# Latent attention taken two heads at a time, with zero-filled rows, a reordered end and an early table load

## The reference

```python
c_q = h_t @ W_DQ + b_DQ
c_kv = h_t @ W_DKV + b_DKV
q_c = (c_q @ W_UQ + b_UQ).reshape(b, s, N_HEADS, D_K).transpose(0, 2, 1, 3)
k_c = (c_kv @ W_UK + b_UK).reshape(b, s, N_HEADS, D_K).transpose(0, 2, 1, 3)
v_c = (c_kv @ W_UV + b_UV).reshape(b, s, N_HEADS, D_K).transpose(0, 2, 1, 3)
q_r = (c_q @ W_QR + b_QR).reshape(b, s, N_HEADS, D_HR).transpose(0, 2, 1, 3)
k_r = (h_t @ W_KR + b_KR)[:, None, :, :]
...
scores = jnp.einsum('bhsd,bhtd->bhst', q, k) * scale
attn = jax.nn.softmax(scores, axis=-1)
o = jnp.einsum('bhst,bhtd->bhsd', attn, v_c)
o = o.transpose(0, 2, 1, 3).reshape(b, s, N_HEADS * D_K)
return o @ W_O + b_O
```

## Time and profile before

| | us |
|---|---|
| median of 3 runs | 893.99 (893.89 to 899.29) |
| profiled execution | 893.57 |
| its span, first to last instruction | 891.9 |
| TensorE busy in the span | 858.8 |
| attention: latent down projection's copies to the last addition | 150.3 to 212.9 |

### The profile page before, as it was taken

The page is one execution under the profiler, slowest core; times in us unless marked ns, Lnnn a source line. Parts: engine busy times, 40 slices in busy tenths (PEclk is TensorE's granted clock), DMA queues, the critical chain, the costliest instruction groups (busy, mean ns, idle before and its releaser), DMA issues.

```text
span 891.9 us, 19675 instructions
## 1 busy us (share of the span) xinstructions
PE 858.8 (96%) x6818; PEld 524.5 (59%) x6818; DVE 595.4 (67%) x1534; ACT 491.3 (55%) x935; POOL 420.2 (47%) x394
## 2 busy tenths in 40 slices
PE   8999999999999999889999999999999999889998
PEld 7888887557567656644444444444444444567656
DVE  2476555664523222878888888888888888379875
ACT  3344443551112122678888888888888888632010
POOL 1332222000241010168888888888888888522000
PEclk9999999999999999999999999999999999999999
DMA  7944497904515613896566655566655562710220
GB/s 241 299 172 161 169 364 279 337 6 154 163 44 83 119 37 140 233 267 137 77 90 88 85 76 76 69 87 87 85 76 76 70 88 96 126 48 1 49 49 24
DMA packets 78391, 109.86 MB, mean 123 GB/s; under 512 B 27036, under 2 KB 64544, under 8 KB 74307
## 3 DMA queue, kind: packets, MB, share of 16 engines
q1 hardware_dynamic: 73019, 93.70, 48.5%
q0 software_dynamic: 4960, 14.96, 4.5%
q10 hardware_dynamic: 360, 0.50, 0.3%
HBM read 86.29 MB, written 21.06 MB: 120 GB/s over the span
## 4 chain that ended last, share of the span: by engine, by line
PE 84%; DVE 7%; SPq 3%; issue 2%; DMA 2%; ACT 2%; ACTq 0%; POOL 0%; DVEq 0%
PE bank L1538 15%; PE bank L1565 14%; PE bank L1512 7%; PE bank L1391 6%; PE bank L1194 5%; PE bank L1181 5%; PE bank L1550 4%; PE bank L1419 3%; PE bank L1800 3%; PE bank L1359 2%; PE bank L1147 2%; PE bank L1277 2%; PE bank L1268 2%; PE bank L1860 2%; SPq L500 1%
## 5 line engine op out<-in xcount | busy, mean ns | idle before, releaser
L759 POOL TENSOR_TENSOR region<-region 128x512 int32<-128x512 int32 x256 | 321.4, 1276 | 61.0 <-ACT region L1042 61.0
L1042 ACT ACTIVATE region<-bank 128x512 f32<-128x512 f32 x512 | 279.6, 596 | 59.9 <-PE bank L1550 48.0
L2287 DVE CUSTOM_DVE_ANT_0 xnT<-bank,region 128x1024 bf16<-128x1024 f32 x128 | 156.1, 1220 | 51.9 <-issue 51.4
L1538 PE MATMUL bank<-region 128*128 (+1 forms) x1024 | 158.5, 276 | 7.7 <-ACT region L1024 5.2
L2287 DVE CUSTOM_DVE_ANT_0 region<-bank,region 128x1024 bf16<-128x1024 f32 x128 | 156.1, 1220 | 0.0
L1538 PEld LDWEIGHTS bank<-region 128*128 128x128 bf16 x1024 | 79.7, 100 | 112.9 <-ACT region L1042 65.2
L1565 PE MATMUL bank<-region 128*32 128x256 f32 x2048 | 139.7, 387 | 0.0
L1565 PEld LDWEIGHTS bank<-region 128*32 128x32 f32 x2048 | 59.1, 109 | 46.9 <-issue 15.6
L706 POOL DMA_DIRECT2D keys_split<-region x48 | 35.8, 748 | 98.2 <-DVE region L2052 98.2
L1512 PE MATMUL bank<-region,xnT 64*128 64x512 bf16 x244 | 73.5, 381 | 0.0
L1514 PE MATMUL bank<-region,xnT 64*128 64x512 bf16 x244 | 73.5, 381 | 0.0
(11 more groups left out here) (395 smaller groups left out, 1324.3 us busy)
## 6 DMA issues: line engine op xcount, KB each, us to landing
region<-keys_split SPq DMA_DIRECT2D x224, 128.0 KB, 5.0
region<-in_ctx SPq DMA_DIRECT2D x32, 512.0 KB, 7.4
keys_split<-region POOLq DMA_DIRECT2D x48, 256.0 KB, 4.1
region<-in_L_ffn_we_gate SPq DMA_DIRECT2D x8, 688.0 KB
region<-in_L_ffn_we_up SPq DMA_DIRECT2D x8, 688.0 KB
region<-in_mask_1x1xSxS_ik SPq DMA_DIRECT2D x1, 4096.0 KB, 16.5
region<-in_L_ffn_we_down SPq DMA_DIRECT2D x8, 512.0 KB
mask_kept<-region SPq DMA_DIRECT2D x1, 2048.0 KB, 9.4
```

Source lines behind the costliest of these rows:

```text
L759: nc.gpsimd.tensor_tensor(out=bits, in0=bits, in1=keep4[k], op=ALU.mult).then_inc(probs_kept, 1)
L1042: nc.scalar.activation(prob4[n % PROBS].rearrange("p a b -> p (a b)"), bank[:, SCORE4[n], :], ACT.Exp, scale=SCALE4).then_inc(exp4_ready, 1)
L1538: last = mm(bank[:, SCORE4[n], k * S:(k + 1) * S], slab[s][:, t * P:(t + 1) * P], qT4[:, bass.ds(u, 1), :].rearrange("p o q -> p (o q)"), ...
L2287: v.tensor_tensor_reduce(out=junk[q], in0=bank[:, 3 + 2 * q:5 + 2 * q, :].rearrange("p a b -> p (a b)"), in1=maskN[:, q, 2 * c * CH:2 * (c ...
```

## The change

Units are numbered anew: a step takes two heads of one batch (`unit2`), so four units are heads 0 and 1 of batch 0, then of batch 1. Rows 65 to 127 of `kvr` and `uT2` and rows 33 to 127 of `cq1` and `fold2` are cleared (GpSimd and ScalarE, near the program's start), and queries and scores multiply all 128 rows. `values2` takes both heads of a step alternately. `TURN2` and `MASKS2` say in which step queries are made and masks turned. VectorE copies turned probabilities a step later than before. At the end, latent outputs are copied per batch, and the first batch's output product comes before the last value products. An exponential of one element on ScalarE makes the table of exponentials load before the down projection's copies.

```diff
 SCORE2 = (6, 7, 4)
+STEPS2 = UNITS2 // 2
+TURN2 = ((2, 3), (), (4, 5), (), (6, 7), (), (), ())
+MASKS2 = ((), (0, 1), (), (2, 3), (), (4, 5), (6,), (7,))
+def unit2(n):
+    return n // 4 * 2 + n % 2, n // 2 % 2
...
             nc.gpsimd.memset(zeros, 0.0).then_inc(setup, 1)
             pool.wait_ge(setup, 4)
+            nc.gpsimd.memset(kvr[COLS2 - 1:P, :], 0.0)
+            nc.gpsimd.memset(cq1[ROWS2 - 1:64, :], 0.0)
+            nc.gpsimd.memset(cq1[64:P, :], 0.0)
+            nc.gpsimd.memset(fold2[ROWS2 - 1:64, :, :], 0.0)
+            nc.gpsimd.memset(fold2[64:P, :, :], 0.0).then_inc(row_blank, 1)
+            pool.wait_ge(row_blank, 1)
             nc.gpsimd.memset(kvr[COLS2 - 1:COLS2, :], 1.0).then_inc(setup, 1)
             pool.wait_ge(setup, 5)
...
                 act.wait_ge(fold2_psum, 2)
+                for r in range(2):
+                    nc.scalar.activation(uT2[r][64:P, :].rearrange("p (a b) -> p a b", b=P),
+                                         ones[64:P, :].unsqueeze(1).broadcast_to([64, T // P, P]), ACT.Copy, scale=0.0)
+                act.wait_ge(row_blank, 1)
                 kept = bank[0:ROWS2, 5, 0:H2 * ROWS2].rearrange("p (h c) -> p h c", c=ROWS2)
                 nc.scalar.activation(fold2[0:ROWS2, :, 0:DCQ], kept[:, :, 0:DCQ], ACT.Copy, scale=SCALE2)
...
+            act.wait_ge(setup, 2)
+            nc.scalar.activation(small[0:1, 7:8], half[0:1, 0:1], ACT.Exp)
             act.wait_ge(in_w2, 16 * N_W2)
             act.wait_ge(setup, 6)
...
-            def values_out(g):
-                act.wait_ge(o2_psum, UNITS2 // 2 * (g + 1))
-                nc.scalar.activation(oT2[:, g, :], bank[:, 5 if g == 0 else 2, :], ACT.Copy).then_inc(o2_ready, 1)
+            def values_out(g, n, c):
+                act.wait_ge(o2_psum, n)
+                nc.scalar.activation(oT2[:, g, c], bank[:, 5 if g == 0 else 2, c], ACT.Copy).then_inc(o2_ready, 1)
             queries_out(0)
             queries_out(1)
             exps(0)
-            for n in range(UNITS2):
-                if n + 1 < UNITS2:
-                    exps(n + 1)
-                if n % 2 == 1 and (n + 3) // 2 < H2:
-                    queries_out((n + 3) // 2)
-                if n % 2 == 0:
-                    mask_out(n // 2)
-                if n == UNITS2 // 2 + 1:
-                    values_out(0)
-            values_out(1)
+            exps(1)
+            for i in range(STEPS2):
+                if i == 0:
+                    queries_out(TURN2[0][0])
+                if i + 1 < STEPS2:
+                    exps(2 * i + 2)
+                for h in TURN2[i][:1] if i else ():
+                    queries_out(h)
+                for g in MASKS2[i][:1]:
+                    mask_out(g)
+                if i + 1 < STEPS2:
+                    exps(2 * i + 3)
+                for h in TURN2[i][1:]:
+                    queries_out(h)
+                for g in MASKS2[i][1:]:
+                    mask_out(g)
+                if i == STEPS2 // 2 + 1:
+                    values_out(0, UNITS2 // 2, slice(0, T))
+            values_out(1, UNITS2 - 2, slice(0, S))
+            values_out(1, UNITS2, slice(S, T))
...
             def queries2(h):
                 pe.wait_ge(u2_ready, h)
-                if h > 1:
-                    pe.wait_ge(maskT_ready, h - 1)
-                mm(bank[0:COLS2, 3, :], fold2[0:ROWS2, h, :], cq1[0:ROWS2, :], start=True, stop=True)\
+                if h >= 4:
+                    pe.wait_ge(maskT_ready, h // 2 * 2 - 2)
+                mm(bank[0:COLS2, 3, :], fold2[:, h, :], cq1, start=True, stop=True)\
                     .then_inc(u2_psum, 1)
             def mask_T(g):
-                pe.wait_ge(u2_ready, min(g + 2, H2))
-                if g > H2 - 2:
+                pe.wait_ge(u2_ready, min(g // 2 * 2 + 4, H2))
+                if g > 0:
...
             def scores(n):
-                h, b = n // B, n % B
+                h, b = unit2(n)
                 if b == 0:
                     pe.wait_ge(u2_ready, h + 1)
                 if n >= 3:
                     pe.wait_ge(exp2, n - 2)
                 for q in range(QT):
                     t = b * S + q * P
-                    last = mm(bank[:, SCORE2[n % 3], q * S:(q + 1) * S], uT2[h % 2][0:COLS2, t:t + P],
-                              kvr[0:COLS2, b * S:(b + 1) * S], start=True, stop=True)
+                    last = mm(bank[:, SCORE2[n % 3], q * S:(q + 1) * S], uT2[h % 2][:, t:t + P],
+                              kvr[:, b * S:(b + 1) * S], start=True, stop=True)
                 last.then_inc(score2, 1)
-            def values2(n):
-                h, b = n // B, n % B
-                r = 32 * (h % 4)
-                pe.wait_ge(pT2_ready, n + 1)
+            def probs_T(n):
+                pe.wait_ge(norm2, n + 1)
+                if n >= 2:
+                    pe.wait_ge(pT2_ready, n - 1)
                 for k in range(2):
-                    last = mm(bank[r:r + DCQ, 5 if h < 4 else 2, b * S:(b + 1) * S], ckv[:, b * QT + k, :],
-                              pT2[n % 2][:, k, :], start=(k == 0), stop=(k == 1), skip_group_check=True)
-                last.then_inc(o2_psum, 1)
+                    for q in range(QT):
+                        last = nc.tensor.transpose(bank[:, n % 2, k * S + q * P:k * S + (q + 1) * P],
+                                                   p2[n % RING2][:, q, k * P:(k + 1) * P], ident[:, :])
+                last.then_inc(pT2_psum, 1)
+            def values2(i):
+                pe.wait_ge(pT2_ready, 2 * i + 2)
+                for k in range(2):
+                    for n in (2 * i, 2 * i + 1):
+                        h, b = unit2(n)
+                        r = 32 * (h % 4)
+                        last = mm(bank[r:r + DCQ, 5 if h < 4 else 2, b * S:(b + 1) * S], ckv[:, b * QT + k, :],
+                                  pT2[n % 2][:, k, :], start=(k == 0), stop=(k == 1), skip_group_check=True)
+                        if k == 1:
+                            last.then_inc(o2_psum, 1)
             pe.wait_ge(cq_ready, 1)
-            mm(bank[0:COLS2, 3, :], fold2[0:ROWS2, 0, :], cq1[0:ROWS2, :], start=True, stop=True).then_inc(u2_psum, 1)
+            mm(bank[0:COLS2, 3, :], fold2[:, 0, :], cq1, start=True, stop=True).then_inc(u2_psum, 1)
             pe.wait_ge(kvr_ready, 1)
             for t in range(TT):
                 last = nc.tensor.transpose(bank[:, 5, t * DCQ:(t + 1) * DCQ], kvr[0:DCQ, t * P:(t + 1) * P],
...
-            for n in range(UNITS2):
-                if n + 2 < UNITS2:
-                    scores(n + 2)
-                if n % 2 == 1 and (n + 3) // 2 < H2:
-                    queries2((n + 3) // 2)
-                if n % 2 == 0:
-                    mask_T(n // 2)
-                pe.wait_ge(norm2, n + 1)
-                if n >= 2:
-                    pe.wait_ge(pT2_ready, n - 1)
-                for k in range(2):
-                    for q in range(QT):
-                        last = nc.tensor.transpose(bank[:, n % 2, k * S + q * P:k * S + (q + 1) * P],
-                                                   p2[n % RING2][:, q, k * P:(k + 1) * P], ident[:, :])
-                last.then_inc(pT2_psum, 1)
-                if n > 0:
-                    values2(n - 1)
-            values2(UNITS2 - 1)
-            pe.wait_ge(o2_ready, 2)
+            for i in range(STEPS2):
+                if i + 1 < STEPS2:
+                    scores(2 * i + 2)
+                    if i > 0:
+                        scores(2 * i + 3)
+                for h in TURN2[i][:1]:
+                    queries2(h)
+                if i == 0:
+                    scores(3)
+                for g in MASKS2[i][:1]:
+                    mask_T(g)
+                if i > 0:
+                    values2(i - 1)
+                for h in TURN2[i][1:]:
+                    queries2(h)
+                probs_T(2 * i)
+                probs_T(2 * i + 1)
+                for g in MASKS2[i][1:]:
+                    mask_T(g)
             for t in range(TT):
+                if t == QT:
+                    values2(STEPS2 - 1)
+                if t % QT == 0:
+                    pe.wait_ge(o2_ready, 2 + t // QT)
                 for g in range(2):
...
                                 AX.X, ALU.max, negate=True).then_inc(nmax2, 1)
-            max2(0)
-            max2(1)
-            for n in range(UNITS2):
+            def norm_probs(n):
                 s = n % RING2
                 dve.wait_ge(exp2, n + 1)
                 link(v.reciprocal(sm2[s][:, 2, :], sm2[s][:, 1, :]))
                 v.tensor_tensor(p2[s], p2[s], sm2[s][:, 2, :].unsqueeze(2).broadcast_to([P, QT, S]), ALU.mult)\
                  .then_inc(norm2, 1)
-                if n + 2 < UNITS2:
-                    max2(n + 2)
+            def probs_out(n):
                 dve.wait_ge(pT2_psum, n + 1)
                 if n >= 2:
-                    dve.wait_ge(o2_psum, n - 1)
+                    dve.wait_ge(o2_psum, n // 2 * 2)
```

(15 more changed lines are left out.)

## The result

The changed kernel took 882.35 us (median of four runs, 881.08 to 886.77) where the kernel before, beside it, took 893.94 (four, 893.11 to 899.29). The ratio is 0.9857, 95% interval 0.9815 to 0.9900; times 893.94 that is 881.2. The profiled execution took 881.08 with a span of 879.4, so 12.49 less than the 893.57 of before. From the start of the copy of the latent keys on VectorE to the end of the second addition ("the attention" from here on) it was 62.54 us before and is 52.22 now.

The account below looks back on a forecast made before the run. TensorE was taken to bound the latent attention, each head costing its matmuls in order, 6.83 us. Gains of 0.3, 6.8 and 3.3 sum to 10.4; 893.57 less that gives 883.2 us, range 881.5 to 888.5.

Parts of the forecast that it names:

- start of the attention to the maximum of unit 4: Head of the latent attention: earlier first maximum and shorter first steps bring unit 4's maximum from 163.45 to 163.15, gain 0.3 us.
- units 4 to 14: Middle of the latent attention: three mask and two query steps take 27.31 us in place of 34.12, gain 6.8.
- end: From unit 14's maximum to the end of the second addition: 11.95 us in place of 15.28, gain 3.3.
- Zero rows: Attention's queries and scores over 128 rows: queries take 0.86 us in place of 1.00, scores neither gain nor lose.
- Values in pairs: Two heads' value products in two column groups overlap: eight records take 0.98 us for two units in place of 1.96.
- Pairs in program order: Rival on value products: strict matmul order needs five slots, not four, 0.22 us more per step; 883.8 us, chance 0.05.
- No overlap of the pairs: Rival on value products: TensorE needs 6.1 us a step and binds again; gain 5.5, time 888.1 us, chance 0.11.
- The ring: VectorE and ScalarE bind the attention's steps: 5.65 us in mask steps, 5.18 in query steps, 4.69 with neither.
- Joints stay: Rival on TensorE's array-form changes: it binds at the old group lengths, 5.85 us a step; 885.2 us, chance 0.10.
- Steps no longer overlap: Rival on attention steps: VectorE's copies wait for the same step's turnings, 8.4 us a step; 898.1 us, chance 0.02.
- End, table, clearing: Attention's end takes 11.95 us from unit 14's maximum; early table load gains 0.15 within the head's 0.3; clearing is hidden.
- the drain of 1.38: Rival on ScalarE's early table load: draining first starts the queries 0.5 us late; 883.7 us, chance 0.02.

Follow-up runs that it names:

- the two runs above: Changed kernel with one head's value products waiting for the end of the other's, 889.97 us; and with values written unit after unit without that wait, 881.59 us.
- the nine kernels of the table: Kernel before, before with zero rows, and changed kernels with 33/65, 33 or 65 rows, serial values, copies between maxima, mask pieces, late table; cross attention 404.07 to 404.21 us.
- before again: Kernel before, unchanged, profiled a second time: 900.39 us, attention 69.83 us, cross attention 403.78 us.
- the second comparison: Both kernels run again unchanged: changed kernel 883.0 us (six runs) against 898.83 us for the kernel before (eleven runs), ratio 0.9831.

## Why the prediction was right about the mechanism and short by two microseconds

The profiled executions can be compared with the working term by term:

| term | predicted | measured |
|---|---|---|
| start of the attention to the maximum of unit 4 | 0.3 | 0.22 (0.79 less the 0.57 by which it started earlier) |
| units 4 to 14 | 6.8 | 34.12 - 27.30 = 6.82 |
| end | 3.3 | 15.28 - 12.01 = 3.27 |
| ahead of the attention | 0 | 0.57 |
| behind it | 0 | 1.58 |

*Zero rows:* right on the joints. Queries gain (0.62 in the changed kernel, 1.95 over sixteen units of the old one), scores have the large form already.

*Values in pairs:* right, 1.06 for eight records against 0.98 to the next group; *Pairs in program order* and *No overlap of the pairs* fall with the two runs above.

*The ring:* right, mask steps 5.66 against 5.65, query steps 5.15 against 5.18. The margin of 0.1 that it left TensorE held for the first maximum alone: behind a query step the second starts 0.83 after the first in place of 0.60, which is hidden because ScalarE still has the first pair of exponentials and the mask copies to do. *Joints stay* falls, since TensorE idles in the steps; *Steps no longer overlap* falls, since the copies don't wait.

*End, table, clearing:* 12.01 against 11.95 from the maximum of unit 14; the load is followed at once, as in the earlier trace rows, so the drain of 1.38 that the Trainium skill ("ScalarE: Activation LUTs", What ACT_TABLE_LOAD costs) adds is not seen here either: 147.64 + 1.28 = 148.92, and the next row starts at 148.93. The root did not move.

**The step that failed** is the frame of the sum: "the sum is made from 893.57", with everything outside the attention carried over unchanged ("all of it moves along"). It was not the same: 0.57 ahead of the attention, where the start varies between 149.74 and 151.12 over the kernels without a fall of the clock ahead of it (why, stays open), and 1.53 in the cross attention. The latter is the fall at 773 us: the nine kernels of the table with 404.07 to 404.21 show such a fall between 760 and 780, the four with 402.54 to 402.65 show none (before again, 403.78, falls at 394 and 797 instead), and the change touches nothing there. Before had one and after none, so the pair shows 2.1 us that belong to chance. With them on top of the 10.32, the profiled run came to 881.08 and the ratio to 881.2, where the range ends at 881.5: that low end took some 5% off the ring and the end, and nothing off the rest. The median of the four runs, 882.35, lies inside it. Most runs of the changed kernel have a mean granted clock below 1 like before: in the second comparison five of six lie at 882.03 to 884.04, about the forecast of 883.2, and the median of 883.0 is 10.2 below the four runs of before near 893.2.

**What was missed altogether** is the second effect of the zero rows, of which I wrote "nothing, neither gain nor loss" for the scores, having read the clock of one execution. In 19 of 39 runs of the kernel before, over the four comparisons, the time lies some 5 to 9 us above the rest. The profiled copy that took 900.39 shows the fall in the attention; for those 19 it is inferred from their time and, in the three comparisons that list it, their mean clock of 0.985 to 0.990 (0.994 to 0.998 in the rest). With 128 rows in the queries, the scores or both no profile shows a fall there, and the 32 runs of the five such kernels that were timed beside them have mean clocks of 0.994 to 1.000. In the first comparison one run of the changed kernel took 886.77, at 0.994 (as the run of 882.46) and without a profile; its cause stays open. Which part a run of before takes sets the ratio: 0.9857 in the first comparison, with one such run in four, 0.9831 in the second, with seven in eleven. The prediction's low end had no room for this either.

Why the clock falls with short rows, and why in about half of the executions only, stays open; rows between 65 and 128 weren't tried.

## What to carry to other kernels

When one engine's order is the whole chain, write down the ring that the other engines will close once it is faster, operation by operation from successive starts in the timeline; here that gave 5.65 and 5.18 for 5.66 and 5.15, and named the next thing to change (the copies' place, 1.28). Before a forecast in tenths is set against a time, look at the granted clock in windows over more than one execution: a fall can be worth most of what the change is (7.3 against 10.3), and can lie in a part that the change never touches. Rows filled with zeros can pay twice, once at the joints of different array forms and once in the clock.

## What the hardware showed that was not expected

- The granted clock fell to 0.50 for 10 and 17 us behind 5 us in which TensorE was busy 5.00 of 5.00, in kernels whose queries and scores had 33 and 65 rows; over 128 rows in either, no profile shows it, though TensorE was as busy (5.00 of 5.00 from 150 to 160 in after).
- Eight records of 128x256 in two column groups, written one group's four behind the other's, took 1.06, the time of four.
- ScalarE's pieces of 64 columns follow each other after 0.104 us, so sixteen of them cost 1.67 where two of 512 cost 0.96.
